# A pre-norm transformer block on one core: b1 loaded ahead of the bias columns, GpSimd's clears behind VectorE's weight splits, W2 issued by ScalarE, new due times

## The reference

```
x = x + attention(layernorm(x))      # causal, 16 heads of 8 channels
x = x + ffn(layernorm(x))
# ffn: 8 experts, 128 -> 512 -> 128
probs    = sigmoid(x @ Wg + bg);  weights = probs * (probs > 0.5)
h        = relu(x @ W1[e] + b1[e])             # for every expert and token
combined = sum_e weights[:, e] * (h @ W2[e] + b2[e])
```

## Time and profile before

| | |
|---|---|
| median of 3 runs | 677.46 us (677.27 to 679.45) |
| the profiled execution's own time | 677.06 us |
| its span, first to last instruction | 675.3 us |
| mean granted clock of TensorE | 0.977 of full speed |
| TensorE busy | 652.4 us, 97% of the span |
| VectorE, ScalarE, GpSimd busy | 450.6, 443.2, 339.1 us |
| DMA traffic | 40.08 MB, mean 59 GB/s |

### The profile page before, as it was taken

One profiled execution on the slowest core, in us unless ns is written; L12 is line 12 of the kernel. 1 busy time (PEld: TensorE's weight loads), 2 busy tenths in 40 slices (PEclk: granted clock), 3 DMA queues, 4 the chain that ended last, 5 costly groups with the idle time before them and its releaser, 6 DMA issues.

```text
span 675.3 us, 12981 instructions
## 1 busy us (share of the span) xinstructions
PE 652.4 (97%) x4325; PEld 439.9 (65%) x4325; DVE 450.6 (67%) x1019; ACT 443.2 (66%) x857; POOL 339.1 (50%) x445
## 2 busy tenths in 40 slices
PE   4989998999999999999999999999999999999998
PEld 3445565667666766667666766666666766677776
DVE  6757786678676876678676876678576776344343
ACT  2446768667766776667776786667666667646543
POOL 5117444457545654457545654456645554554453
PEclk7958999999999999999999999999999999999999
DMA  5441224220322122220322122221322010100200
GB/s 178 97 138 23 57 47 110 58 57 19 92 64 57 48 58 57 73 57 25 93 56 59 48 58 58 73 58 34 79 54 50 31 34 33 49 33 33 79 31 17
DMA packets 24560, 40.08 MB, mean 59 GB/s; under 512 B 3312, under 2 KB 12920, under 8 KB 24496
## 3 DMA queue, kind: packets, MB, share of 16 engines
q1 hardware_dynamic: 24112, 38.89, 20.8%
q10 hardware_dynamic: 384, 0.38, 0.2%
HBM read 23.46 MB, written 2.23 MB: 38 GB/s over the span
## 4 chain that ended last, share of the span: by engine, by line
PE 90%; DVE 3%; ACT 2%; issue 1%; DMA 1%; POOL 1%; SPq 0%; ACTq 0%; DVEq 0%; POOLq 0%
PE ring L1273 11%; PE y_bank L1398 10%; PE ring L1353 10%; PE ring L1206 9%; PE ring L1208 9%; PE ring L1207 9%; PE y_bank L1405 9%; PE y_bank L1400 9%; PE ring L1280 4%; PE ring L1212 3%; DVE f_buf L1174 1%; PE ring L1295 1%; ACT xn L870 1%; PE ring L1369 1%; PE y_bank L1273 1%
## 5 line engine op out<-in xcount | busy, mean ns | idle before, releaser
L969 ACT ACTIVATE h_hi<-ring 128x512 fp32r<-128x512 f32 x256 | 152.6, 599 | 110.4 <-PE ring L1208 106.7
L937 ACT ACTIVATE pt<-ring 128x512 f32<-128x512 f32 x312 | 171.0, 599 | 53.0 <-PE ring L1273 51.1
L845 POOL TENSOR_TENSOR h_lo<-h_all,h_hi 128x512 fp32r<-128x512 f32 x96 | 123.6, 1288 | 161.4 <-ACT h_all L975 143.1
L1161 DVE SCALAR_TENSOR_TENSOR h_lo<-ring,h_hi 128x512 fp32r<-128x512 f32 x160 | 109.1, 685 | 57.1 <-ACT h_hi L969 57.1
L838 POOL TENSOR_SCALAR_AFFINE_SELECT pt<-pt 128x512 f32<-128x512 f32 x128 | 79.8, 637 | 94.5 <-ACT pt L937 94.3
L1094 DVE CUSTOM_DVE_ANT_0 ring<-causal,ring 128x512 f32<-128x512 bf16 x124 | 83.3, 713 | 51.8 <-PE ring L1273 51.8
L1398 PE MATMUL y_bank<-h_hi,w_lo 128*128 128x512 f32 x256 | 110.8, 433 | 2.7 <-DVE f_buf L1174 2.7
L1206 PE MATMUL ring<-x2T_lo,w_hi 128*128 128x512 f32 x256 | 101.9, 398 | 0.0
L1273 PE MATMUL ring<-stack 32*128 32x384 f32 (+3 forms) x998 | 97.1, 372 | 4.9 <-DMA stack<-nmT 2.9
L1208 PE MATMUL ring<-x2T_hi,w_hi 128*128 128x512 f32 x256 | 101.2, 395 | 0.0
L1400 PE MATMUL y_bank<-h_hi,w_hi 128*128 128x512 f32 x256 | 101.2, 395 | 0.0
(11 more groups left out here) (145 smaller groups left out, 795.8 us busy)
## 6 DMA issues: line engine op xcount, KB each, us to landing
f_buf<-gates SPq DMA_DIRECT2D x32, 512.0 KB, 3.7
stack<-parts SPq DMA_DIRECT2D x95, 128.0 KB
x_in<-in_x SPq DMA_DIRECT2D x8, 256.0 KB, 3.0
f_buf<-in_W SPq DMA_DIRECT2D x2, 1024.0 KB, 7.7
out_x<-f_buf SPq DMA_DIRECT2D x7, 256.0 KB, 2.4
stack<-nmT SPq DMA_DIRECT2D x64, 8.0 KB
stack<-stack SPq DMA_DIRECT2D x28, 16.0 KB
out_x<-f_buf SPq DMA_DIRECT2D x2, 128.0 KB, 1.9
```

Of the source, the lines that this page charges most:

```text
L845: g_.tensor_tensor(h_lo[:, (i * SLOTS + s) % H_RING, :], h_all[:], h_hi[:, (i * SLOTS + s) % H_RING, :].bitcast(F32), ALU.subtract).then_i ...
L937: sc.activation(pt[:, slot, :], b[:], ACT.Exp, scale=SCALE).then_inc(free_sem("ex", i, g, u), 1)
L969: sc.activation(h_hi[:, (i * SLOTS + s) % H_RING, :], bank_of("z", i, s)[:], ACT.Relu).then_inc(s_hhi, 1)
L1161: v.scalar_tensor_tensor(out=h_lo[:, (i * SLOTS + s) % H_RING, :], in0=bank_of("z", i, s)[:], scalar=0.0, in1=h_hi[:, (i * SLOTS + s) % H_ ...
```

## The change

Four things are done.

- On ScalarE's queue the three b1 loads are issued ahead of the bias columns (b_cols) and no longer behind them.
- GpSimd's stackset waits until VectorE's splits of the small weights (s_wset at 6) and of b1 (s_b1 at 5) are done; vset stands behind it on GpSimd and so comes later too.
- W2 is issued by ScalarE, behind the last W1 block on TensorE, and no longer by SP.
- Due times (SHIFT) and four costs or dependences in the planner's list are other ones, which gives other orders on all engines.

```diff
-SHIFT = {('act', 'exp', False): 23.0,
-         ('act', 'exp', True): 3.5,
-         ('act', 'nm', False): 15.0,
-         ('act', 'nm', True): -2.5,
-         ('dve', 'klo', False): 4,
-         ('dve', 'merge', False): 8,
-         ('dve', 'merge', True): -2,
-         ('dve', 'qlo', False): 3.0,
-         ('dve', 'smax', False): -4.5,
+SHIFT = {('act', 'exp', False): 25.5,
+         ('act', 'nm', False): 25.0,
+         ('act', 'nm', True): -4.5,
+         ('dve', 'hlo', False): -3,
+         ('dve', 'merge', False): 2,
+         ('dve', 'merge', True): -2.0,
+         ('dve', 'smax', False): -5.0,
          ('dve', 'smax', True): -4,
-         ('dve', 'w1', False): 4.0,
-         ('dve', 'xT', False): 5.0,
-         ('dve', 'yT', True): 7.5,
+         ('dve', 'w1', False): 3.5,
+         ('dve', 'xT', False): 10.0,
          ('pe', 'ex', False): 3.0,
-         ('pe', 'ex', True): -11.5,
          ('pe', 'gate', False): -11.0,
          ('pe', 'k', False): 4.5,
-         ('pe', 'max', False): 12.5,
+         ('pe', 'max', False): 17.0,
+         ('pe', 'max', True): 3.0,
          ('pe', 'pv', False): 4.0,
          ('pe', 'q', False): 3.0,
+         ('pe', 'q', True): 6,
          ('pe', 'v', False): 4.5,
-         ('pe', 'w1', False): 0.5,
+         ('pe', 'w1', False): 6.0,
...
-         ('pool', 'nm', False): 10.5}
+         ('pool', 'causal', False): -4,
+         ('pool', 'causal', True): 9.5}
...
-    put("dma", ("b1", None), -60.5, 600, ("dma", ("wqkv", None)))
-    put("dma", ("w1", 0), -60, 2500, ("dma", ("b1", None)))
+    put("dma", ("b1", None), -60.5, 1200, ("dma", ("wqkv", None)))
+    put("dma", ("w1", 0), -60, 1900, ("dma", ("b1", None)))
...
-    put("sp", ("w2load", None), -8.9, 600, ("pe", ("w1", EXPERTS - 1)))
-    put("dma", ("w2", None), -8, 9000, ("sp", ("w2load", None)))
+    put("act", ("w2load", None), -8.9, 700, ("pe", ("w1", EXPERTS - 1)))
+    put("dma", ("w2", None), -8, 9000, ("act", ("w2load", None)))
...
-    put("pool", ("stackset", 1), -20, 2200, ("pool", ("rs1", 0)))
+    put("pool", ("stackset", 1), -20, 2200, ("pool", ("rs1", 0)), ("dve", ("wqk", None)))
...
-                elif kind == "w2load":
-                    sp.wait_ge(*full("w1", EXPERTS - 1))
-                    sp.dma_start(w2_in[:].rearrange("p a (c d) -> p (a c) d", d=C),
-                                 w2.rearrange("e (c p) d -> p (e c) d", p=P)).then_inc(s_w2, 16)
...
                 elif kind == "stackset":
+                    pool.wait_ge(s_wset, 6)
+                    pool.wait_ge(s_b1, 5)
                     g_.memset(stack_half(1), 1.0).then_inc(s_stackset, 1)
...
             act.dma_start(wqkv_in[:], w_qkv).then_inc(s_wqkv, 16)
-            act.dma_start(b_cols[:], b_cols_in).then_inc(s_bcols, 16)
             act.wait_ge(s_b1zero, 1)
             for k in range(3):
                 act.dma_start(b1_in[32 * k:32 * k + EXPERTS, :], b1).then_inc(s_b1load, 16)
+            act.dma_start(b_cols[:], b_cols_in).then_inc(s_bcols, 16)
...
+                elif kind == "w2load":
+                    act.wait_ge(*full("w1", EXPERTS - 1))
+                    act.dma_start(w2_in[:].rearrange("p a (c d) -> p (a c) d", d=C),
+                                 w2.rearrange("e (c p) d -> p (e c) d", p=P)).then_inc(s_w2, 16)
```

## The result

The changed kernel took 674.78 us in the median of six runs (672.2 to 676.9), the kernel before 678.04 us beside it on the same chip. The ratio is 0.9945 with an interval of 0.9921 to 0.9969: faster by 0.55%, some 3.7 us, where 9.6 us were forecast. Ratios are taken from fast runs alone, which leaves out two runs of "W2 in four pieces" (679.5 and 680.7 us) and two of "W2 late alone" (677.3 and 678.7) that are in the medians given. For most kernels whose runs lie apart a ratio is nearer to the quotient of the means than to that of the medians. The profiled execution of the changed kernel was its lowest run (672.2 us, span 670.5, mean clock 0.99), so the profiles show 4.9 us where the medians show 3.3 and the ratio 3.7.

What follows compares the result with a forecast made beforehand. Ahead of 60 us TensorE's waits and half clock bound the kernel; from 104.7 us, fixed matmul work does. Gains of 3.1 + 3.5 + 3.0 = 9.6 us, due times 0, gave 667.9 us, range 659 to 675.

Steps and rivals of the forecast that it cites:

- part 2: Ahead of the first exp scores: with W2 off SP's queue the maxima's transfers land sooner, -3.5 us (gains of 1.5 to 4.4).
- part 3: TensorE's half clock in the head: less of it once waits shrink, -2.5 and -0.5 us, bounds 0 and -9.
- part 1: Up to W1's first matmul: GpSimd's clears stop blocking b1's conversion and b1 lands sooner, -3.1 us, bounds -2.3 and -4.4.
- part 3, earlier half-clock stretch: Half clock that began in the first 20 us: 3 us less idle TensorE inside it, -0.5 us.
- part 3, second half-clock stretch: TensorE's 15.6 us at half clock from 41.8 on: up to 7.8 us could go, -2.5 us taken.
- part 4: New due times on all engines: 0, bounds -5 and +5 for later sequences, -1 and +2 for the first.
- the small transfers stand behind it in one queue: Step on the maxima's DMA: their 8 KB transfers wait because 2 MB of W2 precede them in SP's queue; -3.5 us.
- Rival D: Second gain not had: maxima transfers crawl beside W2 (1.5 us gain) or exp scores wait (+1); 673.9 us, chance 0.17.
- the wait belonged to the same stretch: Argument against the clock staying down: TensorE's wait before the exp scores lay in the half-clock stretch begun at 36 to 38.
- the sign: Check on TensorE's granted clock between 40 and 60 us: it should be above 0.57.
- Rival B: The clock stays down for as many microseconds as before though both stalls go; 670.9 us, chance 0.18.
- my own signs: Checks: exp scores at 34 to 36 us, first z near 95; wrong if first z comes no sooner than 101.

Runs made afterwards that it cites:

- W2 in four pieces: The changed kernel with ScalarE issuing W2 as four 512 KB transfers instead of one of 2 MB; 677.33 us, ratio 0.9949.
- W2 late alone: The kernel before with only W2's issue moved, on SP, to right behind the first group's maxima transfers; 674.88 us, ratio 0.9922.
- clears alone: The kernel before with only the two waits in front of GpSimd's stackset clears added; 673.59 us, ratio 0.9945.
- the edit alone: The kernel before with only W2 issued by ScalarE instead of SP; 677.84 us, ratio 0.9999.
- change, W2 late: The changed kernel with W2 issued by SP right behind the first group's maxima transfers, not by ScalarE ahead of them; 671.49 us, ratio 0.989.
- W2 back on SP: The changed kernel with W2 issued by SP again instead of ScalarE; 675.25 us, ratio 0.9964.
- the maxima by GpSimd: The changed kernel with the first group's two maxima transfers issued from GpSimd's queue; 674.69 us, ratio 0.9951.
- b1 first: The kernel before with only the b1 loads issued ahead of the bias columns; 677.36 us, ratio 0.9986.
- due times alone: The kernel before with only the changed kernel's due times (SHIFT); 679.35 us, ratio 1.0015.
- the filled pair: 16 more warm matmuls in TensorE's waits, W2 behind first maxima: old due times, clears moved, b1 early 663.5 us (0.9791); changed kernel's orders 671.45 us (0.989).

## Why the prediction was wrong

The median of 674.8 us lies at the edge of the range of 659 to 675, and the gain was 3.3 to 3.7 us, not 9.6. Two steps failed: the landing of part 2, priced at 3.5 us and worth 0.33, and the tie in part 3 between the wait and the clock. In the profiles, term by term:

| term | forecast | profiles |
|---|---|---|
| part 1, to the first W1 matmul | -3.1 | -3.25 |
| part 2, W2's issue to the exp scores | -3.5 | -0.33 |
| part 3, earlier half-clock stretch | -0.5 | -2.52 |
| part 3, second half-clock stretch | -2.5 | about -1.0 (estimate) |
| part 4, the due times | 0 | about +2.2 (estimate) |

The two estimates divide the +1.24 us between the exp scores and the first z: 1.9 us less at half clock (15.6 and 13.7) is worth about half of that, and the remainder goes to the order.

**Part 1 was right** in mechanism and size. The conversion took 422 ns, the first W1 matmul came at 10.81 (forecast about 10.95), and clears alone give 11.39 (forecast 11.38 for the clears). The landing gained 0.6 us, not 1.2, which was enough. The clears alone have the ratio of the whole change. The rule of the Trainium skill, "SBUF — State Buffer", section "SBUF: two separate sides", has one engine of the pair block while the other's instruction holds it; the trace agrees and shows more of it: the conversion was held not by one memset but by three in a row, and when it started sooner it grew to 3652 ns. The conversion at 7.90 didn't slow GpSimd's pow (6.55 to 7.60), since b1 landed just behind it.

**Part 2 failed at the landing: "the small transfers stand behind it in one queue".** The issues did fall, from 3.95 to 1.19 us. The landing stayed at W2's end, whichever way the queues were shared out, and the edit alone gave 0.9999. Of the 2.85 us that after gains between W1's first matmul and the exp scores, 2.52 come from W1's blocks being done sooner (W2's issue follows 15.09 us after the first W1 matmul, not 17.61) and 0.33 from the landing, where the sum had 3.5. I took the bias columns' 5.3 us as an upper bound. But the bias columns were issued at 1.28 us, W1 at 1.30, so W1's 2 MB weren't ahead of them, and the row was no bound for a transfer issued behind 2 MB; in the changed kernel, where they are issued behind W1, they took 6.3 us. b1's own landing, 5.62 us from ScalarE's queue behind W1 in SP's, was the nearer row. The view of DMA issues had the one that mattered, W2's own landing, here for before and for after (median us from issue to landing; the 0.5 KB of the view isn't W2's size, which is 2 MB):

```profile
f_buf<-in_W SPq DMA_DIRECT2D x1, 0.5 KB, 11.0
```

```profile
f_buf<-in_W ACTq DMA_DIRECT2D x1, 0.5 KB, 10.5
```

W2 lands at 42.7 and 36.4, and the maxima land within a microsecond ahead of it, at 41.74 and 35.64, with either issuer. The Trainium skill, "DMA: Bandwidth & Descriptors", section "Queues, rings and completion order", has the engines take packets in turn from the queue rows; a landing near the first end of the range would follow. Here the measurement decides against that landing, though it doesn't show what the engines did in between: 6.2 to 6.4 us from the second issue to the landing with W2 in another queue, and 3.5 to 3.7 us from the first issue to the exp scores where W2 came behind and TensorE wasn't late itself. Rival D named this failure ("the small transfers crawl beside W2") at 673.9 and 0.17; it was the nearest of the five, though its 1.5 us of landing gain were still more than there was.

**Part 3 failed at the step "the wait belonged to the same stretch".** Half clock went from two stretches (9.6 to 19.8 and 36.9 to 57.4 us) to one (36.6 to 50.2), and the clock in 40 to 60 us from 0.57 to 0.74, as the sign asked. But from the exp scores to the first z the time grew by 1.2 us where 2.5 were to come off. In the changed kernel the wait was still there, 3.43 us ahead of 35.68. With the wait gone the clock stayed down just as long: 20.5 us at half clock in "W2 late alone", 20.5 in before, and 17 us in "change, W2 late". Rival B had this right. The earlier stretch was mis-sized the other way, 0.5 us for 2.5. W2's issue follows the first W1 matmul by 15.04 to 15.09 us in the three kernels in which TensorE had full clock throughout (after, W2 back on SP, the maxima by GpSimd), by 16.3 with some 3 us of half clock behind that matmul (clears only, b1 first) and by 17.61 with 5.8 (before), so half clock costs about half of its length there. The exp scores met their sign by this, and by luck, not by the landing. What the runs showed besides: the clock is worth some 7.5 us in this head, and which of two levels a run takes varies from run to run of one program. A term for it belongs in the range, not in the sum.

**Part 4** was right behind the first z: 570.1 to 570.6 us in all kernels of the table. In the head, due times alone read +1.0 us (0.15%), which its interval doesn't tell from nothing, inside the bounds of -1 and +2. With W2 late the new due times go with a longer time, some 6.7 us (0.989 against 0.9791 in the filled pair), outside these bounds. Most or all of it comes with the clock, as the runs above show. Which key does it, and how, stays open; the exp keys of sequence 0 and the waits that were filled are excluded as the main cause.

By my own signs: the first z at 99.91 was sooner than 101, but 5 us later than the 95 forecast, and the exp scores at 35.68 lay inside their 34 to 36 for another reason than the one given. The sign for the clock in 40 to 60 us was met too, though its term failed: it asked for less half clock in a fixed window, and not for fewer microseconds up to the first z.

## What to carry to other kernels

A small transfer on the critical path has to be issued ahead of a large one that can wait; another queue didn't help it here. Where the wait of an issue goes away, ask what its landing waits for: issue and landing have to be priced together. Before a memset is placed on GpSimd, look for a VectorE conversion from SBUF beside it. A station that every variant shares (here the first z) separates head from steady state at once. Before a difference between two orders is put down to the order, compare their microseconds at half clock.

## What the runs showed of the hardware

- Two transfers of 8 KB issued 2.7 to 3 us behind one of 2 MB were used 9.8 to 10.3 us after the large one's issue, in the same queue, with the large one in ScalarE's, and with the small ones in GpSimd's; issued ahead of it, 3.5 to 3.7 us after their own first issue.
- One VectorE conversion of 72x512 took 422 ns free, 3093 beside GpSimd's memsets and 3652 when it started sooner beside them; it ended 0.27 to 0.28 us behind the second large memset in five kernels.
- Four 512 KB issues on ScalarE took 4.96 us together, one of 2 MB 0.83.
- The same program on one core ran at two levels, 662 to 664 and 670 to 671 us, with mean clocks of 1.00 and 0.98. Neither level could be chosen by filling TensorE's waits.
- The clock fell at 46.3 us behind 0.33 us of idle time in one kernel and held through 2.6 us of it, spread over 20 to 60 us, in another; once down it stayed so with TensorE busy, for 13.7 us in the changed kernel and for 20.5 us in "W2 late alone".
